# A graph network's edge stages laid out in 128 streams along the partitions

## The reference

```python
# layer 0: attention; a softmax per dst over its incoming edges, then a weighted sum
aij = (x[dst] - x[src]) @ (w2_W.T @ a) + a @ w2_b
m = segment_max(aij, dst); aexp = exp(aij - m[dst])
res = segment_sum((aexp / segment_sum(aexp, dst)[dst])[:, None] * (x[src] @ w2_W.T + w2_b), dst)
x = layernorm(x + res + x @ w1_W.T + w1_b)
# layer 1: three rounds of x = segment_sum(x[src], dst) / max(count, 1), averaged
x = layernorm(x + mean_rounds(x))
# layer 2: a small network judges every edge, a node keeps the best message
h = relu(concat([x[src], x[dst], edge_attr]) @ W1 + b1)      # 96 -> 64
v = h @ W2 + b2                                              # 64 -> 32
x = layernorm(x + maximum(segment_max(v, dst), x))
# layer 3: three rounds of normalised sums over the edges, averaged
x = layernorm(x + norm_rounds(x))
```

## Time and profile before

| | us |
|---|---|
| three runs | 15086.85, 15105.52, 15144.85 (median 15105.52) |
| the profiled execution | 15086.83, span 15085.1 |
| busy over the span: PE, DVE, ACT, POOL | 9136.6, 7557.0, 5428.7, 8453.2 |
| attention, first to last gather | 546 to 5492 |
| until finish_attention's first gather | 5529.9 (37 later) |
| mean rounds end | 7682 |
| judging, first to last gather | 7817.4 to 12965.5 |
| until finish_judging's first gather | 12990.7 |
| finish_judging's last gather | 13119 |

### The profile page before, as it was taken

One profiled execution on the slowest core, in us unless ns is written; L12 is line 12 of the kernel. 1 busy time (PEld: TensorE's weight loads), 2 busy tenths in 40 slices (PEclk: granted clock), 3 DMA queues, 4 the chain that ended last, 5 costly groups with the idle time before them and its releaser, 6 DMA issues. The chain is left out here.

```text
span 15085.1 us, 283012 instructions
## 1 busy us (share of the span) xinstructions
PE 9136.6 (61%) x103161; PEld 7201.5 (48%) x103161; DVE 7557.0 (50%) x8053; ACT 5428.7 (36%) x8098; POOL 8453.2 (56%) x7439
## 2 busy tenths in 40 slices
PE   2255555555555536898935555555555555398987
PEld 1244444444444436898832222222222222298987
DVE  2366666666666647676632222222222222466666
ACT  1244444444444434565521111111111111165654
POOL 5687777777777771221355555555555555421312
PEclk8555555555555558999965555555555555599999
DMA  4222322222222227898932222222222222398987
GB/s 81 45 88 86 88 88 88 86 88 86 88 87 86 88 62 266 318 355 321 336 105 49 50 50 50 49 50 50 49 51 49 50 50 49 86 355 321 353 317 277
DMA packets 1982697, 1995.93 MB, mean 132 GB/s; under 512 B 1212295, under 2 KB 1680825, under 8 KB 1982521
## 3 DMA queue, kind: packets, MB, share of 16 engines
q1 hardware_dynamic: 1445721, 1664.66, 32.7%
q0 software_dynamic: 239424, 185.44, 7.0%
q10 hardware_dynamic: 297504, 145.26, 3.7%
HBM read 1615.99 MB, written 381.61 MB: 132 GB/s over the span
## 5 line engine op out<-in xcount | busy, mean ns | idle before, releaser
L654 POOL DMA_INDIRECT attend_and_count_rows<-table,attend_and_count_ring x3136 | 3933.4, 1254 | 1075.2 <-issue 999.4
L1302 POOL DMA_INDIRECT judge_edges_rows<-table,judge_edges_ring x3128 | 2958.6, 946 | 2198.9 <-ACT judge_edges_ring L1451 1222.4
L689 PE MATMUL attend_and_count_counts<-attend_and_count_hot_hi,attend_and_count_hot_lo 128*128 128x98 bf16 x15680 | 1478.8, 273 | 2302.0 <-ACT attend_and_count_stage L799 1389.3
L1412 DVE TENSOR_TENSOR_SCAN judge_edges_feat<-judge_edges_keep,judge_edges_feat,judge_edges_p_feat 32x512 f32<-32x512 bf16 x782 | 960.1, 1265 | 3513.6 <-remote 2720.1
L1205 POOL DMA_INDIRECT base<-slot_sums,last_slot x588 | 987.0, 1678 | 2943.1 <-DMA slot_sums<-propagate_mean_whole 1417.3
L689 PEld LDWEIGHTS attend_and_count_counts<-attend_and_count_hot_hi,attend_and_count_hot_lo 128*128 128x128 bf16 x15680 | 1208.7, 134 | 2571.1 <-ACT attend_and_count_stage L799 1462.5
L1365 PE MATMUL judge_edges_p_hid<-judge_edges_feat,judge_edges_w 96*128 96x512 f32 x1564 | 1340.9, 1007 | 1363.1 <-ACT judge_edges_feat L1447 650.6
L799 ACT CAST attend_and_count_stage<-attend_and_count_counts 128x784 uint8<-128x784 f32 x1960 | 1533.6, 811 | 1045.1 <-PE attend_and_count_counts L689 548.8
L1112 PE MATMUL propagate_mean_p_dense<-propagate_mean_split,propagate_mean_part 128*128 128x96 bf16 x36456 | 1658.0, 208 | 303.9 <-ACT propagate_mean_part L1009 234.6
L1112 PE MATMUL propagate_norm_p_dense<-propagate_norm_split,propagate_norm_part 128*128 128x96 bf16 x36456 | 1665.5, 208 | 233.3 <-ACT propagate_norm_part L1009 155.3
L1112 PEld LDWEIGHTS propagate_mean_p_dense<-propagate_mean_split,propagate_mean_part 128*128 128x128 f16 x36456 | 1635.9, 100 | 311.7 <-ACT propagate_mean_part L1009 234.7
(11 more groups left out here) (255 smaller groups left out, 11467.5 us busy)
## 6 DMA issues: line engine op xcount, KB each, us to landing
propagate_mean_raw<-matrix SPq DMA_DIRECT2D x372, 1568.0 KB, 8.7
propagate_norm_raw<-matrix SPq DMA_DIRECT2D x372, 1568.0 KB, 8.8
matrix<-attend_and_count_stage SPq DMA_DIRECT2D x245, 784.0 KB
scan<-attend_and_count_out SPq DMA_DIRECT2D x784, 68.0 KB
inject<-attend_and_count_zeros SPq DMA_DIRECT2D x196, 256.0 KB
attend_and_count_rows<-table,attend_and_count_ring POOLq DMA_INDIRECT x3136
judge_edges_rows<-table,judge_edges_ring POOLq DMA_INDIRECT x3128
judge_edges_rows<-inject SPq DMA_DIRECT2D x782, 64.0 KB
```

What stands on the lines that cost most here:

```text
L654: nc.gpsimd.indirect_dma_start(out=rows[:, u, g, j, :], out_offset=None, in_=D.table0[:, :], in_offset=rows_of(ring[:, u, g, j:j + 1])).th ...
L689: last = nc.tensor.matmul(counts[:, r % 2, k // 4, NH * (k % 4):NH * (k % 4) + NH], hot_lo[:, u, slot, :], hot_hi[:, u, slot, :], start=Tr ...
L1302: nc.gpsimd.indirect_dma_start(out=rows[:, u, half, j, 0:FEAT], out_offset=None, in_=D.table2[:, :], in_offset=rows_of(ring[:, u, half, j: ...
L1412: last = nc.vector.tensor_tensor_scan(out=feat[2 * FEAT:WIDE, u, half], data0=keep[2 * FEAT:WIDE, u, half], data1=p_feat[2 * FEAT:WIDE, u, ...
```

## The change

The edges are cut into 128 streams of 3125 consecutive edges, one per partition. A gather fetches the next edge of every stream, so that scans run along the free dimension in the layout in which the gather puts the rows, one scan per feature.

- Attention: 49 turns of up to 64 gathers, 3125 in all; the table has 33 words a node. VectorE does one scan for the maximum and 33 scans of 64 for the sums; the weights for `keep` lie in PSUM. No transposes; TensorE only counts. Five of a turn's ten compares stand ahead of the attention of the turn before, one within it, four behind. One store per turn.
- Judging: 391 steps of 8 edges per stream, a ring of 16 steps, VectorE's and SP's work in quads of four steps. POOL waits for the turning of 16 steps ago. `hold` is 32 scans of 32 edges from SBUF to SBUF, `top` 32 scans whose messages lie in PSUM; `send` is four matmuls with the hidden block as weights, so nothing is turned back. `keep` and `neg` are loaded whole at the start; SP issues two loads a quad.
- The tails of the streams are joined after each of the two stages: a short chain over PE, DVE and ACT, a gather of each stream's first end and a scatter that puts the joined row back, ahead of the 98 gathers. The joining operations per slice go.
- `src` is loaded by one transfer in place of 12; the row placed for the second half goes; the semaphores of the first stages are cleared after the attention, with a barrier.

```diff
 # attend_and_count, POOL
+            def gather(b, u, uses, many=BATCH):
+                before = pool.snap(pool.to_reg(uses))
+                listings = pool.snap(pool.to_reg(b + 1))
+                pool.wait_ge(begun, 1)
+                pool.wait_ge(used[u], before)
+                pool.wait_ge(listed, listings)
+                for j in range(many):
+                    nc.gpsimd.indirect_dma_start(out=rows[:, u, j, :], out_offset=None, in_=D.table0[:, :],
+                                                 in_offset=rows_of(ring[:, u, j:j + 1])).then_inc(gathered[u], 16)
+
+            with pool.Fori(0, TURNS // 2) as i:
+                for u in range(2):
+                    gather(i * 2 + u, u, i)
+            gather(TURNS - 1, 0, TURNS // 2, rest)
 
 # attend_and_count, VectorE
+            def scan_sums(b, u, uses, many):
+                keep, weight = p_keep[:, u, 0:many], gain[:, u, 0:many]
+                dve.wait_ge(weighed, b * 2 + 2)
+                nc.vector.tensor_tensor(value[:, 0:many], rows[:, u, 0:many, 0:FEAT],
+                                        weight.unsqueeze(2).to_broadcast([P, many, FEAT]), ALU.mult).then_inc(v, 1)
+                dve.wait_ge(scanned, b)
+                dve.wait_ge(out_stored[u], uses * 16)
+                nc.vector.tensor_tensor_scan(out=out[:, u, 0:many, FEAT], data0=keep, data1=weight,
+                                             initial=out[:, 1 - u, BATCH - 1, FEAT:FEAT + 1], op0=ALU.mult, op1=ALU.add)
+                dve.wait_ge(v, b * V + 4)
+                for f in range(FEAT):
+                    last = nc.vector.tensor_tensor_scan(out=out[:, u, 0:many, f], data0=keep, data1=value[:, 0:many, f],
+                                                        initial=out[:, 1 - u, BATCH - 1, f:f + 1], op0=ALU.mult, op1=ALU.add)
+                    if f == 0:
+                        last.then_inc(used[u], 1)
+                last.then_inc(scanned, 1)
+
+            def attend(b, u, uses, between, many=BATCH):
+                scan_scores(b, u, uses, many)
+                between()
+                scan_sums(b, u, uses, many)
+
+            for m in range(COUNT_SUBS):
+                compare(0, m)
+
+            def one(t, i, odd):
+                for m in EARLY:
+                    compare(t, m)
+                attend(t - 1, odd, i, lambda: compare(t, LATE[0]))
+                for m in LATE[1:]:
+                    compare(t, m)
+
+            over_turns_after_first(dve, one)
+            attend(TURNS - 1, 0, TURNS // 2, lambda: None, rest)
+            dve.wait_ge(scanned, TURNS)
+            dve.wait_ge(topped, TURNS)
+            nc.vector.tensor_copy(S.tail[:], out[:, 0, rest - 1, :])
 
...
 # finish_attention, POOL
+            nc.gpsimd.indirect_dma_start(out=ends[:], out_offset=None, in_=D.scan0[:, :],
+                                         in_offset=rows_of(S.first_end[:, 0:1])).then_inc(ends_gathered, 16)
+            pool.wait_ge(joined, 1)
+            nc.gpsimd.indirect_dma_start(out=D.scan0[:, :], out_offset=rows_of(S.first_end[:, 0:1]),
+                                         in_=whole[:], in_offset=None).then_inc(ends_placed, 16)
+            pool.wait_ge(ends_placed, 16)
             for h in range(NH):
                 nc.gpsimd.indirect_dma_start(out=last[:, h, :], out_offset=None, in_=D.scan0[:, :],
...
 # judge_edges, POOL
+            def gather(it, u):
+                q, j = divmod(u, QUAD)
+                listings = pool.snap(pool.to_reg(it * QUADS + (q + 1)))
+                turns = pool.snap(pool.to_reg(it * QUAD + (j + 1)))
                 pool.wait_ge(begun, 1)
                 pool.wait_ge(listed, listings)
-                for half in range(HALVES):
-                    for j in range(LANES):
-                        nc.gpsimd.indirect_dma_start(out=rows[:, u, half, j, 0:FEAT], out_offset=None, in_=D.table2[:, :],
-                                                     in_offset=rows_of(ring[:, u, half, j:j + 1])).then_inc(gathered[u], 16)
-
-            with pool.Fori(0, STEPS // 2) as i:
-                for u in range(2):
-                    gather(i * 2 + u, u)
-            gather(STEPS - 1, 0)
+                pool.wait_ge(turned[q], turns)
...
 # judge_edges, SP
+            def load(it, q, many=EACH):
+                first = it * (RING * STEP) + q * EACH
+                turns = sp.snap(sp.to_reg(it * QUAD + QUAD))
+                holds = sp.snap(sp.to_reg(it * QUADS + (q + 1)))
                 sp.wait_ge(begun, 1)
...
-            load(STEPS - 1, 0, STEPS // 2, (CHUNK, last_edges))
+                sp.wait_ge(turned[q], turns)
+                sp.wait_ge(held, holds)
+                sp.dma_start(inject[:, q % 2, 0:many], along_streams(D.inject[0:N_EDGES, :])[:, stretch(first, many), :]).then_inc(loaded[q], 16)
+                sp.dma_start(rows[:, q * QUAD:(q + 1) * QUAD].rearrange("p s l w -> p (s l) w")[:, 0:many, FEAT:2 * FEAT],
...
 # judge_edges, TensorE
+            def turn(it, u):
+
+                q, j = divmod(u, QUAD)
+                pe.wait_ge(copied, it * RING + u)
+                pe.wait_ge(held, it * QUADS + (q + 3))
+                pe.wait_ge(gathered[u], it * (16 * STEP) + 16 * lanes_of(it, u))
+                for lane in range(STEP):
+                    last = nc.tensor.transpose(p_feat[:, lane * P:(lane + 1) * P], rows[:, u, lane, :], S.ident[:])
+                last.then_inc(turned[q], 1)
+
...
+            def send(it, u):
+
+                q, j = divmod(u, QUAD)
+                pe.wait_ge(rectified, it * RING + (u + 1))
+                if j == 0:
+                    pe.wait_ge(topped, it * QUADS + (q + 1))
+                for lane in range(LANES):
+                    last = nc.tensor.matmul(p_msg[:, q % 2, j, :, lane, :], hidden[:, u % 2, lane * P:(lane + 1) * P], w2[:],
+                                            start=True, stop=True)
+                last.then_inc(sent, 1)
+
+            def one(it, u):
+                turn(it, u)
+                send(*before(it, u))
+                lift(it, u)
 
...
 # judge_edges, VectorE
+            def hold(it, q, many=EACH):
+
+                first = it * (RING * STEP) + q * EACH
+                dve.wait_ge(held, it * QUADS + (q + 2))
+                dve.wait_ge(turned[q], it * QUAD + QUAD)
+                dve.wait_ge(loaded[q], it * 32 + 32)
+                here = rows[:, q * QUAD:(q + 1) * QUAD].rearrange("p s l w -> p (s l) w")
+                there = rows[:, (q - 1) % QUADS * QUAD + QUAD - 1, STEP - 1]
+                for f in range(FEAT):
+                    last = nc.vector.tensor_tensor_scan(out=here[:, 0:many, 2 * FEAT + f], data0=keep[:, stretch(first, many)],
+                                                        data1=inject[:, q % 2, 0:many, f], initial=there[:, 2 * FEAT + f:2 * FEAT + f + 1],
                                                         op0=ALU.mult, op1=ALU.add)
-                last.then_inc(held[u], 1)
-
...
+            def top(it, q, many=EACH):
+
+                first = it * (RING * STEP) + q * EACH
+                steps = QUAD if many == EACH else LAST - QUAD
+                dve.wait_ge(topped, it * QUADS + (q + 2))
+                dve.wait_ge(stored[q % 2], it * (QUADS // 2 * 16) + q // 2 * 16)
+                dve.wait_ge(sent, it * RING + (q * QUAD + steps + 1))
+                messages = p_msg[:, q % 2].rearrange("p s h l f -> p (s h l) f")
+                for f in range(FEAT):
+                    last = nc.vector.tensor_tensor_scan(out=best[:, q % 2, 0:many, f], data0=neg[:, stretch(first, many)],
+                                                        data1=messages[:, 0:many, f], initial=best[:, 1 - q % 2, EACH - 1, f:f + 1],
+                                                        op0=ALU.add, op1=ALU.max)
+                last.then_inc(topped, 1)
+
+            def turn_of(it):
+                for q in range(QUADS):
+                    ahead = q + 2
+                    last = isinstance(it, int) and q == QUADS - 1
+                    hold(it + ahead // QUADS, ahead % QUADS, rest if last else EACH)
+                    top(it, q)
+
+            for q in range(2):
+                hold(0, q)
+            with dve.Fori(0, TURNS - 1) as it:
+                turn_of(it)
+            turn_of(TURNS - 1)
+            top(TURNS, 0)
```

831 lines of the change are left out of this document (381 added, 450 removed).

## The result

The changed kernel takes 15,409.4 us (median of four runs, 15,370.6 to 15,451.3) where the kernel before takes 15,102.1 (four runs). It is slower by 1.9%: ratio 1.019, 95% interval 1.0167 to 1.0213. The profiled execution took 15,414.6 us, its span is 15,412.8, 327.7 longer than before's.

A forecast was written before the change was run, and what follows sets the result against it. POOL's gather issue was taken to bound the attention, and other engines' lateness during its bursts to slow judging; -205 - 10 + 5 - 5 - 65 - 5 + 9 - 384 + 12 = -648 from 15086.8 gave 14,440 us, range 13,550 to 15,500.

The forecast's parts named there:

- What bounds the kernel now.: Attention: POOL bounds it, 965 us lost to stretched gathers; judging: other engines get late after some 4 us of unbroken issue.
- In runs of nine pairs back to back ... 1.5 a pair, 735 us: Attention: 490 compares, now bunched, each pair stretches two gathers from 2.5 to 4.0 us, adding 735 us.
- -205 forecast: Attention's gathers: sum of terms 4740 us for 4946, bounds 0 and -320.
- VectorE's own load per turn stays under POOL's 96: Attention: 40 us of compares plus 33 scans of 64 elements a turn stay under POOL's 96 us.
- A step is then 10.0 us of burst, its first 4 undisturbed, 6.0 at a loss of 0.62: 8.2 + 3.7 = 11.9: Judging: TensorE's 8.2 us of work plus 3.7 lost while POOL gathers; 12.2 us a step with holds and waits.
- 384: Judging: 391 steps of 12.2 us plus 20 make 4790 us for 5174, a gain of 384.
- Rival 1: Judging: POOL alone bounds it, 3976 us, -1198 in place of -384, total 13,625; chance 0.30.
- Rival 2: Judging slower: POOL's pauses too short to free the others, 14.7 us a step, 5768 us, total 15,420; chance 0.22.
- The hold scans: Judging: 3,128 scans with two SBUF inputs stretch gathers they meet, 50 us in all, 0.1 a step.
- The lock of 470 us: Judging: one SBUF lock over each run of 32 holds would add 470 us; not taken, single scans assumed.
- The end of the attention: finish_attention: ends 10 to 25 us after its last gather instead of 90; net -65 us (-30 to -80).
- 16 steps deep, so no single late result stops POOL: Judging: the ring hides single late results, but when it fills POOL waits a little at each step.

The follow-up runs named there:

- e5: Kernel after, with the attention's ten compares per turn spread, one per 6 gathers: 14,975.1 us, ratio 0.991 to the kernel before; attention 4982 us.
- e9: Kernel after with compares spread and a 128x1024 POOL memset per 8 judging gathers: 13,965.6 us on the chip where the kernel before takes 13,643.6.
- e17: Kernel after with compares spread and a 128x2048 POOL memset per 8 judging gathers: 14,496.0 us, 0.960 of the kernel before; judging 4571 us.

## Why the prediction was wrong

1. *What bounds the kernel now.* The lateness was read rightly as coming from POOL's unbroken issue. But I applied it only to judging. The earlier trace rows showed the attention's gathers stretched, and I booked this as loss alone (965 us); it was also what kept the mean pitch there at 1.58 us, above the 1.46 at which judging is free. e5, with 1.59 and no run of more than 13 unstretched gathers, has no late casts and no stands.
2. *"In runs of nine pairs back to back ... 1.5 a pair, 735 us".* This is the step that failed: -205 forecast, +460 measured, 665 of the 976 us between forecast and result. The sum priced the bunched compares by the gathers that they stretch, and the unbroken gathers between the bunches at nothing. With bunched compares 1648 of the 3125 gathers lie in unstretched runs of more than 20, up to 68 long (before none was longer than 19); the counting nearly stops in the longest of them, falls behind, and every fourth turn POOL stands 52 us. *"VectorE's own load per turn stays under POOL's 96"* is true of its work and not of its time. Where the 5406 go: 3906 of bare pitch, (1227 - 946) x 3125 = 878 of stretching, 624 of standing.
3. *"A step is then 10.0 us of burst, its first 4 undisturbed, 6.0 at a loss of 0.62: 8.2 + 3.7 = 11.9".* This is the second step that failed: with the 43 us at its end judging gained 76 us, not 384. POOL doesn't wait a little at each step; it waits once a quad, for the ring list (L1438), after 40 us of burst. Nor is the loss the same all along. TensorE's last turning in one burst, and its next lifting:

```profile
10029.91 1.04 PE L1339 MATMUL judge_edges_p_feat<-ident,judge_edges_rows 128*96 128x128 f32 x8
...
10064.62 3.78 PE L1346 MATMUL judge_edges_p_hid<-judge_edges_feat,judge_edges_w 96*128 96x512 f32 x4 [10.29 <-ACT judge_edges_feat L1449]
```

This burst goes from 10018.58 to 10058.2. TensorE turns steps freely in its first 12 us, then does one sending until 6 us after its end. Over all bursts 2.8 of a quad's 4 turnings start in the first 16 us and 0.3 in the other 24. TensorE's own work was also too high in the sum: 1896.5 us for the 7548 matmuls of some 377 steps are 5.0 a step, not 8.2, since two of three liftings ran at the full clock (1.98 us each, granted 1.00 from 10018 to 10026) and the rest at half of it (3.78, granted 0.50 from 10011 to 10016). With 5.0 and one window of 4 us a quad the forecast's formula gives (4 x 5.0 + 36 x 0.62) / 4 = 10.6; measured are 12.9. So neither its 8.2 nor its 4 and 0.62 hold, and that their errors partly cancel is luck.
4. Rival 1, "POOL alone bounds judging", is what happens on the odd chip. No trace of one chip can tell this: for the kernel before it is worth 15,100 against 13,644 us. What the unchanged kernel after takes there wasn't measured. An estimate from e9, whose memsets take judging from 3976 (rival 1's working) to 4241: 13,966 - 265 = 13,700 with spread compares, about level with the kernel before (13,644).
5. Rival 2 has nearly the measured total (15,420), but by the wrong sum: judging got 119 faster, and the attention made the loss. Its mechanism, that the ring lets POOL run on and so takes the others' windows, is right in part for judging (POOL's stands fell from 1297 to 1148 us, yet some 12 us of each burst stay free), and stronger in the attention, where no rival of mine stood. That 15,409 lies inside my range of 13,550 to 15,500 is luck too. POOL's stand comes at 12 us per 32 gathers, not at 2 or 4 per 8.
6. The hold scans stretched next to nothing (a gather lasts 946 ns before and after; the 1680 that overlap a scan last 949, the others 943: 9 us for 50 forecast). The lock of 470 us that I had derived from the page "SBUF — State Buffer" of the Trainium skill (section "SBUF: two separate sides") did not appear: this trace does not agree with it for scans of 0.28 us.
7. The end of the attention was right. The last gather and the last slice's result:

```profile
6109.44 0.94 POOL L881 DMA_INDIRECT finish_attention_last<-scan,last_edge  x1 [0.30 <-issue]
```

```profile
6117.82 0.62 DVE L824 TENSOR_TENSOR x_sb<-work,stat 128x448 f32<-128x448 f32 x1
```

8 us after the last gather instead of 91 (before, the last result is at 5746.4 and the last gather ends at 5655.15); from the stage's first gather to its result 143.6 for 216.5 us, -73 for -65 forecast. The mean rounds that follow took 32 us more; no run explains it.
8. *"16 steps deep, so no single late result stops POOL"*: the depth is paid back at the end, when 14 steps are left over, +43 us. Where nothing is late (e9 on the odd chip, e17 on a common one) this stretch is 20 us.

## What to carry to other kernels

Where GpSimd issues indirect gathers in a long run, look at the gaps of the *other* engines and divide them by the number of instructions in them: if each takes the same time, far more than its work, then try the pitch of the gathers. Here a slower issue (work of GpSimd's own between them, other work spread evenly over them) made the whole faster, by 0.8% to 4% against the kernel before. A stall that two engines inflict on each other can be what a third one lives on, so bunching it was not free here. Try such a kernel on more than one chip before tuning to this.

## What the runs showed of the hardware

- In a long run of indirect gathers at 1.25 us, ScalarE hears of TensorE's count matmuls only every 22.40 us for 8 matmuls with their 8 loads, and every 44.80 for 16 with 16 (1.40 us an instruction), and VectorE's hold scans come one per 1.40 us. In judging it sets in some 12 us into a burst. In judging at a pitch of 1.35 us (memsets counted in) it is still there, at 1.46 POOL never stands for it. Fetching 32 bytes of a row or 128 makes no difference in judging (5027 and 5029 us). The cause inside the chip stays open.
- Of five chips whose number is known, four behave so. On the fifth the kernel before takes 13,644 us instead of 15,080 to 15,115.
- Empty instructions on POOL, 8 a gather, left the pitch of the gathers at 1.25 us, and so did a loop of two laps per 8 gathers. A memset that waits for the one before does make a break: the memset of 128x1024 takes 0.97 us, that of 128x2048 1.82.
